# Two graph layers on one core: the additions X + H move from between the layers into layer two, and the offsets come first

## The chip, the cores and the metric

One core of a Trainium2 chip runs the whole program. The metric is the device time of one execution in microseconds (us); the kernel before takes 1938.24 us as the median of 3 runs (1938.19 to 1938.62).

## What is computed

3125 nodes with 160 features each (64 scalars, 32 vectors of three), 103125 edges sorted by target. Each of two layers does

```
h = relu(layernorm(x))
x = x + layer(h, edges)
```

Layer one makes a message per edge from the row h[src], the edge's four values and weights from a small network over 64 edge features, sums the messages by target, and applies node matrices and gates. Layer two is

```
out0 = C0 * (ss * e0 @ W1 + dot * INV3 @ W2)      # ss, vv: the rows h[src]
out1 = C1 * (p3 + p4 + p5)
m_agg = segment_sum(concat(out0, out1), dst)
x = x + relu([m_agg_s @ Ws, m_agg_v @ Wv])
```

What matters here is the residual of layer two: the result is X + H + relu(...) in the kernel's terms, where X is the sum after layer one without h, and H is relu(layernorm(X)), because layer two's own input h is added to its output.

## The kernel before, in words

All arithmetic is in float32. Nodes lie in 25 tiles of 128; `X` and `H` are 128 x 25 x 160 in SBUF. Edges are cut into 116 turns (the code's groups) of seven tiles of 128 edges, the last turn holding one. Four turns make an iteration; layer two runs two leading iterations (turns 0 to 7), written out, and then nine periods of three iterations.

For every edge tile the rows of the source nodes have to be brought into `g`. There are three ways. Most tiles are fetched from a table in HBM by an indirect DMA whose descriptors GpSimd (POOL) writes, from indices in SBUF (line 704, one per tile). Some seventh tiles are made by TensorE: VectorE compares node numbers with the wanted ones (lines 819 and 824, `compare`), TensorE multiplies the resulting 0/1 tiles with `H` (line 1003, `find`, 25 matmuls), ScalarE copies the result (line 745). A few are fetched row by row by SyncE and ScalarE (line 612).

In layer two a turn is then: VectorE builds the selection (lines 802 and 806, `select`), TensorE sums seven tiles (line 992, `aggregate`), VectorE turns the result (line 877, `turn`), and once in four turns TensorE applies the layer's matrix (line 1013, `lin2`) and VectorE adds to `acc` at an offset read from `place_i` (line 891, `accumulate`). The gather of turn s waits for the aggregation of turn s-4, the aggregation waits for its gathers in two parts (four tiles, then the rest), and `sel` has two buffers. VectorE's order in a stage is select, compare for two turns ahead, turn of the turn before, accumulate. If the targets of a turn span more than a window of 32 nodes, the layer is passed over again.

Between the layers (`vector_mid`, line 1097) VectorE, ScalarE, TensorE and POOL work tile by tile on layer one's node results (lines 1063, 1082, 1106, 1109, 1152, 1117), then statistics, roots and the normalised `H` (lines 1122, 286, 288, 1132, 1136 on VectorE; line 293 on ScalarE for tiles 0 to 11). SyncE writes `H` to the table in eight pieces as they come (line 1161), and POOL's first gather of layer two waits for all eight. VectorE goes on, after its last piece of `H`, with X = X + H in two parts (lines 1139 and 1141), the offsets of the windows (`windows`, lines 429, 432 and 433: `rel`, `place`, `place_i`), and the products of the weight tables (lines 1146 and 1147), for which TensorE waits before it composes layer two's matrix (line 1072). Then layer two begins on VectorE.

The tail (`vector_tail`, line 1174) adds relu of the aggregated result to `X` and stores it.

Of the kernel before, what the change touches and what calls it, by code (L numbers as in the profile page):

```python
# [28 lines left out]
ALU = mybir.AluOpType  # L29
# [4 lines left out]
P = 128  # L34
N = 3125
E = 103125
NT = -(-N // P)
# [40 lines left out]
ROOT_AT = (4, 10, 14)  # L78
ROOTS = (0, 18, NT)
BY_ACT = 12  # L80
PIECES = ((0, 2), (BY_ACT, 15), (2, 5), (15, 18), (5, 8), (18, 22), (8, BY_ACT), (22, NT))
THIRD = 3

# [18 lines left out]
def build(nc, x, node_vec, src_idx, src_rows0, src_rows1, src_by_row, node_id, dst_idx, edge_sh, edge_feat, ident, iota, lin_sc, lin_sc_scale,  # L102
# [7 lines left out]
    with ctx:  # L110
        def sb(name, shape, dt=F32):
            return ctx.enter_context(nc.sbuf_tensor(name, shape, dt))
# [4 lines left out]
        def sem(name):  # L117
            return ctx.enter_context(nc.semaphore(name))
# [6 lines left out]
        X = sb("X", [P, NT, D])  # L125
        H = sb("H", [P, NT, D])
# [15 lines left out]
        pool_sb = sb("pool_sb", [P, 2])  # L142
        eps_col = sb("eps_col", [P, 1])
        warm = sb("warm", [P, 1])
        ident_sb = sb("ident_sb", [P, P])
        iota_sb = sb("iota_sb", [P, WIN])
        node_id_sb = sb("node_id_sb", [P, NT])
# [79 lines left out]
        edge_set = sem("edge_set")  # L227
# [13 lines left out]
        h1_ready = sem("h1_ready")  # L241
        h1_by_dve = sem("h1_by_dve")
        scaled = sem("scaled")
        rows1_out = sem("rows1_out")
        added = sem("added")
        weights_ready = sem("weights_ready")
        comp_done = sem("comp_done")
        comp_copied = sem("comp_copied")
# [6 lines left out]
        by_dve = [tiles for tiles in pieces if tiles[0] >= BY_ACT]  # L255
# [170 lines left out]
        def windows(then):  # L426

            wide = [P, GROUPS, TILES]
            then(nc.vector.tensor_tensor(rel[:].rearrange("p (g t) -> p g t", t=TILES),
                                         dst[:].rearrange("p (g t) -> p g t", t=TILES),  # L430
                                         first[:].unsqueeze(2).to_broadcast(wide), ALU.subtract))
            then(nc.vector.tensor_copy(place[:], first[0:1, :]))
            then(nc.vector.tensor_copy(place_i[:], place[:]))
# [58 lines left out]
        def edge_layer(layer):  # L492
            L = f"l{layer}_"
            own_weights = layer == 0
# [298 lines left out]
            def vector(dve):  # L793
# [78 lines left out]
                def turn(f, o, s):  # L872
                    dve.wait_ge(agg_done, UNROLL * f + (o + 1))
                    if o % UNROLL == 0 and s != 0:

                        dve.wait_ge(lin2_done, f)
                    nc.vector.transpose(turned_all[:, o % UNROLL, 0:planes, :].rearrange("p c n -> p (c n)"),  # L877
                                        sums[:, o % 2, 0:width]).then_inc(turn_done, 1)
# [14 lines left out]
                def stage(f, it, o, s, p, e, k):  # L893
                    if s == 0:
                        dve.wait_ge(node_id_in, 16)
                        compare(f, p, e, PICKED[layer][0], 0, 0, True)
                    if s is None or s < GROUPS:
                        select(f, it, o, s)
                        if pick_after(o, s, p, 2):
                            compare(f, p, e, (o + 2) % UNROLL, *pick_after(o, s, p, 2), s is not None and s + 2 < UNROLL)  # L900
                        if s == GROUPS - 2:
                            accumulate(f, it, range(UNROLL), 0)
                        if own_weights:
                            products(f, it, o, 0, s, p, e)
                            if tiles_of(s) == TILES:
                                products(f, it, o, 1, s, p, e)
                            if o == UNROLL - 1 and s != GROUPS - 1:
                                if s == GROUPS - 1 - UNROLL:
                                    dve.wait_ge(named_in[layer], 16 * f + 32)
                                    dve.sem_inc(named_read, 1)  # L910
                                    dve.sem_inc(match_done, 1)
                                else:
                                    compare(f, p, e, 2, 0, 1, False)
                    if s is None or 1 <= s <= GROUPS:
                        turn(f, o - 1, None if s is None else s - 1)
                    if s == GROUPS:
                        nc.vector.tensor_scalar(rel[:], rel[:], float(WIN), None, ALU.subtract)
                        nc.vector.tensor_scalar(place[:], place[:], float(WIN), float(NPAD), ALU.add, ALU.min)
                    if o >= UNROLL:
                        if o == UNROLL + 1:  # L920
                            accumulate(f, it, range(UNROLL), 1)
                    elif o >= 2 and (s is None or UNROLL <= s < GROUPS - 2):
                        accumulate(f, it, range(2 * (o - 2), 2 * (o - 2) + 2), 0)

                with passes(dve) as r:
                    stages(dve, r, stage, GROUPS + 2)
                    pass_over(dve, r)

                    dve.drain()
                    nc.vector.tensor_copy(place_i[:], place[:])  # L930
                    dve.drain()

# [162 lines left out]
                nc.scalar.activation(big1_sb[:, m, :], banks[:, m % BANKS, 0:D], ACT.Copy).then_inc(comp_copied, 1)  # L1095

        def vector_mid(dve):
            n = 0
            for t in range(NT + 2):
                if t < NT:  # L1100
                    pre = banks[:, t % BANKS, :]
                    dve.wait_ge(node0_done, t + 1)
                    dve.wait_ge(sig_ready, t + 1)
                    if t >= BANKS:
                        dve.wait_ge(x_ready, t - BANKS + 1)
                    nc.vector.scalar_tensor_tensor(out=val[:, t % BANKS, 0:S_CH], in0=pre[:, 0:S_CH],
                                                   scalar=a_col[:, t:t + 1], in1=sig[:, t % BANKS, 0:S_CH],
                                                   op0=ALU.mult, op1=ALU.mult)
                    nc.vector.scalar_tensor_tensor(
                        out=val[:, t % BANKS, S_CH:D].rearrange("p (c i) -> p c i", i=3),  # L1110
                        in0=pre[:, S_OUT:PRE].rearrange("p (c i) -> p c i", i=3), scalar=a_col[:, t:t + 1],
                        in1=sig[:, t % BANKS, S_CH:S_OUT].unsqueeze(2).to_broadcast([P, V_CH, 3]),
                        op0=ALU.mult, op1=ALU.mult).then_inc(val_ready, 1)
                u = t - 2
                if u >= 0:
                    dve.wait_ge(x_ready, u + 1)
                    last = nc.vector.bn_stats(stats[:, u, :], X[:, u, :])
                    if u == parts[n][-1]:
                        last.then_inc(stats1_step, 1)
                        dve.wait_ge(stats1_step, n + 1)  # L1120
                        for v in parts[n]:
                            last = nc.vector.bn_aggr(mean_var[:, v, :], stats[:, v, :])
                        last.then_inc(var1_step, 1)
                        n += 1
            n = 0
            for i, own in enumerate(by_dve):
                if n < len(parts) and own[-1] >= parts[n][0]:
                    invert(dve, parts[n], n, root1_done, norm1_step, norm1_ready)
                    n += 1
                    dve.wait_ge(norm1_ready, n)  # L1130
                for u in own:
                    last = nc.vector.tensor_scalar(H[:, u, :], X[:, u, :], rstd[:, u:u + 1], shift[:, u:u + 1], ALU.mult, ALU.add)
                last.then_inc(scaled, 1)
                dve.wait_ge(scaled, i + 1)
                at = slice(own[0], own[-1] + 1)
                nc.vector.tensor_scalar(H[:, at, :], H[:, at, :], 0.0, None, ALU.max).then_inc(h1_by_dve, 1)
            assert n == len(parts)
            dve.wait_ge(h1_by_dve, len(by_dve))
            nc.vector.tensor_tensor(X[:, BY_ACT:, :], X[:, BY_ACT:, :], H[:, BY_ACT:, :], ALU.add).then_inc(added, 1)
            dve.wait_ge(h1_ready, BY_ACT)  # L1140
            nc.vector.tensor_tensor(X[:, 0:BY_ACT, :], X[:, 0:BY_ACT, :], H[:, 0:BY_ACT, :], ALU.add).then_inc(added, 1)
            dve.wait_ge(acc1_clear, 2)
            then = Steps(dve, edge_set)
            windows(then)
            dve.wait_ge(pair_in, 64)
            nc.vector.tensor_tensor(pair[:], pair[:], pair_k[:], ALU.mult)
            nc.vector.tensor_tensor(wout[:], wout[:], wout_k[:], ALU.mult).then_inc(weights_ready, 1)
# [251 lines left out]
```

## Time and profile before

| | us |
|---|---|
| median of 3 runs | 1938.24 |
| lowest, highest | 1938.19, 1938.62 |
| the profiled execution's own time | 1939.32 |
| span of the trace | 1937.5 |
| TensorE busy (matmul) | 1791.9 |
| POOL busy | 1408.5 |
| VectorE busy | 1371.9 |

The trace's times count from the span's start. Layer one fills it up to about 1011 us, the part between the layers up to about 1045 us, layer two the rest. Busy time of POOL counts the writing of descriptors (0.95 us for a gather), not the 0.30 us that follows each.

### The profile page before, as it was taken

Reading aid. Unit: us, or ns where it says so; the run is one execution under the profiler, and the core shown is the slowest. Engines: PE = TensorE matmul, PEld = TensorE weight load, DVE = VectorE, ACT = ScalarE, POOL = GpSimd, SP = SyncE. Lnnn points to the kernel's source line nnn. Section 1 sums busy time; section 2 is a strip of 40 time slices with the busy share of each in tenths; the row PEclk is TensorE's granted clock in tenths of the full one; section 3 lists DMA queues with packets and bytes.
Section 4 is the critical chain, followed back from the end, with each engine's and each line's share of the span. In section 5 each row is a group of like instructions: output and inputs, shape, how many; then the busy total and the mean of one; then the engine's idle time right before and its main releaser. Section 6 shows DMA issues by size and latency. Waiting matters only on the chain.

```text
span 1937.5 us, 55467 instructions
## 1 busy us (share of the span) xinstructions
PE 1791.9 (92%) x16896; PEld 1559.4 (80%) x16896; DVE 1371.9 (71%) x2793; ACT 174.6 (9%) x402; POOL 1408.5 (73%) x1505
## 2 busy tenths in 40 slices
PE   6989889898989899898975999999999999999998
PEld 4767666676767676676654899999999999999998
DVE  5878787878787878787778556666565665656654
ACT  5100001010010001010122000000000000000000
POOL 1777777777777777777755777777777777777774
PEclk9999999999999989899986999999999999999999
DMA  6333333434334343434323333233333323333233
GB/s 239 103 101 104 103 104 103 104 93 109 98 103 105 103 104 103 105 92 114 102 70 82 77 73 77 72 77 73 77 75 73 76 72 76 73 76 76 73 77 91
DMA packets 110902, 179.67 MB, mean 93 GB/s; under 512 B 30046, under 2 KB 78460, under 8 KB 110460
## 3 DMA queue, kind: packets, MB, share of 16 engines
q0 software_dynamic: 70656, 120.68, 26.1%
q1 hardware_dynamic: 35288, 53.34, 8.7%
q10 hardware_dynamic: 4644, 2.19, 0.5%
q8 instruction: 108, 1.77, 0.4%
q14 instruction: 206, 1.69, 0.3%
HBM read 169.95 MB, written 6.14 MB: 91 GB/s over the span
## 4 chain that ended last, share of the span: by engine, by line
POOL 49%; PE 23%; issue 18%; DVE 4%; DMA 3%; ACTq 2%; DVEq 1%; POOLq 0%; ACT 0%
POOL g L704 49%; PE w_ps L1003 12%; PE sums L992 4%; PE sums L1013 2%; DMA g<-node_table,src 2%; ACTq L612 1%; DVE work L858 1%; PE sums L1003 1%; PE sums L988 1%; PE w_ps L956 1%; DVE work L852 1%; PE w_ps L481 1%; PE sums L460 1%; PE hid_ps L942 1%; ACTq L609 0%
## 5 line engine op out<-in xcount | busy, mean ns | idle before, releaser
L704 POOL DMA_INDIRECT g<-node_table,src x1472 | 1394.0, 947 | 479.7 <-issue 464.3
L1003 PE MATMUL w_ps<-H,work 128*128 128x160 f32 x2900 | 405.5, 300 | 1.5 <-issue 1.5
L1003 PEld LDWEIGHTS w_ps<-H,work 128*128 128x128 f32 x2900 | 399.2, 191 | 1.9 <-issue 1.9
L858 DVE TENSOR_TENSOR work<-w_ps,g 128x384 f32<-128x384 f32 (+3 forms) x693 | 297.8, 457 | 87.6 <-DMA g<-node_table,src 47.7
L956 PE MATMUL w_ps<-fc_sb,work 64*128 64x224 f32 x1612 | 238.0, 394 | 90.8 <-DVE work L852 78.4
L877 DVE STREAM_TRANSPOSE turned<-sums 128x160 f32<-128x160 f32 x232 | 79.3, 342 | 306.9 <-PE sums L1013 201.8
L988 PEld LDWEIGHTS sums<-work,sel 128*32 128x32 f32 x6448 | 203.6, 114 | 112.9 <-issue 70.1
L956 PEld LDWEIGHTS w_ps<-fc_sb,work 64*128 64x128 f32 x1612 | 172.7, 199 | 137.8 <-DVE work L852 104.8
L806 DVE TENSOR_TENSOR sel<-mixed,sh 128x896 f32<-128x896 f32 x232 | 251.4, 1084 | 26.6
L988 PE MATMUL sums<-work,sel 128*32 128x160 f32 x6448 | 255.5, 311 | 0.0
L992 PE MATMUL sums<-g,sel 128*128 128x160 f32 x1612 | 237.5, 301 | 6.6 <-DMA g<-node_table,src 4.9
L992 PEld LDWEIGHTS sums<-g,sel 128*128 128x128 f32 x1612 | 224.7, 190 | 10.0 <-DMA g<-node_table,src 3.8
L824 DVE TENSOR_TENSOR work<-mixed,node_id_sb 128x3200 f32<-128x3200 f32 x58 | 202.5, 3491 | 4.5
L824 DVE TENSOR_TENSOR acc<-mixed,node_id_sb 128x3200 f32<-128x3200 f32 x55 | 192.0, 3491 | 8.6 <-PE w_ps L1003 4.6
L1003 PE MATMUL sums<-H,acc 128*128 128x160 f32 x1400 | 198.1, 302 | 0.0
L1003 PEld LDWEIGHTS sums<-H,acc 128*128 128x128 f32 x1400 | 191.8, 191 | 7.9 <-issue 7.9
L1003 PE MATMUL w_ps<-H,acc 128*128 128x160 f32 x1350 | 187.8, 299 | 0.0
L1003 PEld LDWEIGHTS w_ps<-H,acc 128*128 128x128 f32 x1350 | 184.2, 190 | 0.0
L852 DVE TENSOR_TENSOR work<-w_ps,g 128x256 f32<-128x256 f32 x462 | 155.7, 377 | 0.0
L942 PE MATMUL hid_ps<-feat,fc_sb 128*128 128x512 f32 x232 | 145.5, 712 | 1.5 <-issue 1.5
L1013 PE MATMUL sums<-turned,big_sb 128*80 128x128 f32 (+1 forms) x1044 | 125.8, 275 | 0.9 <-DVE turned L877 0.9
L1013 PEld LDWEIGHTS sums<-turned,big_sb 128*80 128x80 f32 (+1 forms) x1044 | 116.6, 156 | 8.5 <-issue 7.0
(85 smaller groups left out, 650.1 us busy)
## 6 DMA issues: line engine op xcount, KB each, us to landing
g<-node_table SPq DMA_DIRECT2D x2304, 0.6 KB
feat<-edge_feat_dram SPq DMA_DIRECT2D x60, 512.0 KB
g<-node_table,src POOLq DMA_INDIRECT x1472
g<-node_table ACTq DMA_DIRECT2D x1152, 0.6 KB
named<-src_rows_dram SPq DMA_DIRECT2D x30, 192.0 KB
X<-x_dram SPq DMA_DIRECT2D x5, 400.0 KB, 7.1
node_table<-H SPq DMA_DIRECT2D x5, 400.0 KB, 2.7
named<-src_rows_dram SPq DMA_DIRECT2D x30, 64.0 KB
```

What stands on the lines that cost most here:

```text
L704: nc.gpsimd.indirect_dma_start(out=g[:, slot(p, u, j), :], out_offset=None, in_=table[layer], in_offset=bass.IndirectOffsetOnAxis(ap=src[: ...
L806: nc.vector.tensor_tensor(sel[:, o % 2, 0:n, :].rearrange("p t (k n) -> p t k n", k=4), hot[:, 0:n, :].unsqueeze(2).to_broadcast([P, n, 4, ...
L824: nc.vector.tensor_tensor(match[layer][i], wanted.unsqueeze(1).to_broadcast(wide), node_id_sb[:].unsqueeze(2).to_broadcast(wide), ALU.is_e ...
L852: return nc.vector.tensor_tensor(blocks(at), w[:, :, h * S_CH:(h + 1) * S_CH].rearrange("p t (m c) -> p t m c", m=2), rows[:, :, 0:S_CH].r ...
L858: nc.vector.tensor_tensor(blocks(at), w[:, :, 2 * S_CH + j * V_CH:2 * S_CH + (j + 1) * V_CH].unsqueeze(2).to_broadcast([P, n, m, V_CH]), r ...
L877: nc.vector.transpose(turned_all[:, o % UNROLL, 0:planes, :].rearrange("p c n -> p (c n)"), sums[:, o % 2, 0:width]).then_inc(turn_done, 1)
L942: nc.tensor.matmul(hid_ps[:], fc1_sb[:], feat[:, half, within * HID:(within + 1) * HID], start=True, stop=True).then_inc(hid_done, 1)
L956: last = nc.tensor.matmul(w_ps[:, h, part[2 * h + j] - a, 0:W_N], hid[at, o % 2, (2 * h + j) * P:(2 * h + j + 1) * P], fc2_sb[at, :], tile ...
L988: last = nc.tensor.matmul(sums[at, o % 2, 0:width].rearrange("p (m n) -> p m n", n=WIN), sel[:, o % 2, j, at], row, tile_position=(0, k * ...
L992: last = nc.tensor.matmul(sums[:, o % 2, 0:D], sel[:, o % 2, j, :], g[:, slot(p, o % UNROLL, j), :], **first_last)
L1003: last = nc.tensor.matmul(found_at[:, i, 0:D], match[layer][i][:, t, :], H[:, t, :], start=(t == 0), stop=(t == NT - 1))
L1013: last = nc.tensor.matmul(lin_ps[:, r, :].rearrange("p (u n) -> p u n", n=WIN), big[:, m, r * rows_of:(r + 1) * rows_of], turned_all[:, :, ...
```

## The change

`windows` is moved from the end of `vector_mid` to its start, followed by a memset of a new 128 x 1 tile `once` to 1. The two additions and their waits leave `vector_mid`. In layer two's stages 5 (tiles 12 to 24) and 6 (tiles 0 to 11), behind `turn`, VectorE does X = H * once + X with one scalar_tensor_tensor each. At the end of every pass over layer two `once` is set to 0, so that a second pass would add nothing.

```diff
+X_AND_H = {5: range(BY_ACT, NT), 6: range(BY_ACT)}
...
                     if s is None or 1 <= s <= GROUPS:
                         turn(f, o - 1, None if s is None else s - 1)
+                    if not own_weights and s in X_AND_H:
+                        tiles = X_AND_H[s]
+                        if tiles[0] == 0:
+                            dve.wait_ge(h1_ready, BY_ACT)
+                        else:
+                            dve.wait_ge(h1_by_dve, len(by_dve))
+                        dve.wait_ge(once_set, 1)
+                        nc.vector.scalar_tensor_tensor(out=X[:, tiles[0]:tiles[-1] + 1, :], in0=H[:, tiles[0]:tiles[-1] + 1, :],
+                                                       scalar=once[:, 0:1], in1=X[:, tiles[0]:tiles[-1] + 1, :],
+                                                       op0=ALU.mult, op1=ALU.add).then_inc(added, 1)
...
                     dve.drain()
+                    if not own_weights:
+                        nc.vector.memset(once[:], 0.0).then_inc(once_set, 1)
                     nc.vector.tensor_copy(place_i[:], place[:])
                     dve.drain()
...
         def vector_mid(dve):
+            windows(Steps(dve, edge_set))
+            nc.vector.memset(once[:], 1.0).then_inc(once_set, 1)
             n = 0
...
-            dve.wait_ge(h1_by_dve, len(by_dve))
-            nc.vector.tensor_tensor(X[:, BY_ACT:, :], X[:, BY_ACT:, :], H[:, BY_ACT:, :], ALU.add).then_inc(added, 1)
-            dve.wait_ge(h1_ready, BY_ACT)
-            nc.vector.tensor_tensor(X[:, 0:BY_ACT, :], X[:, 0:BY_ACT, :], H[:, 0:BY_ACT, :], ALU.add).then_inc(added, 1)
             dve.wait_ge(acc1_clear, 2)
-            then = Steps(dve, edge_set)
-            windows(then)
             dve.wait_ge(pair_in, 64)
```

## Rows read from the trace of the kernel before

**Rows 1.** Chain that ended last, 1036 to 1100: start us, us, what
```profile
1036.82 2.94 DMA node_table<-H
...
1040.60 1.68 POOL g L704
...
1096.56 2.53 DMA g<-node_table,src
1099.13 0.90 PE sums L992 x2
```

**Rows 2.** Line 704 from 1040 to the end: duration ns min/median/max, first and last start
```profile
L704 POOL DMA_INDIRECT g<-node_table,src x703: 942/946/1682, 1040.6 to 1919.3; - x176
  issue: 212.5, 697
```

**Rows 3.** PE timeline: start, us, engine, line, operation [idle before <- releaser]
```profile
1044.70 5.67 PE L1072 MATMUL w_ps<-wout,pair 128*128 128x160 f32 x20 [17.74 <-DVE wout L1147]
...
1081.82 2.17 PE L992 MATMUL sums<-g,sel 128*128 128x160 f32 x14 [1.74 <-DMA g<-node_table,src]
...
1096.80 1.32 PE L992 MATMUL sums<-g,sel 128*128 128x160 f32 x8 [1.93 <-DMA g<-node_table,src]
```

**Rows 4.** PE timeline, the end of layer two
```profile
1918.15 3.97 PE L992 MATMUL sums<-g,sel 128*128 128x160 f32 x28
1922.33 0.51 PE L992 MATMUL sums<-g,sel 128*128 128x160 f32 x2 [0.21 <-DMA g<-node_table,src]
```

**Rows 5.** Windows: us, PE, PEld, DVE, ACT, POOL busy, PE clock, DMA share, GB/s
```profile
1098.00:1105.00 7.00, 6.00 (x23) 5.87 (x23) 6.10 (x8) 0.00 (x0) 5.48 (x6) 0.51 0.31 74
```

**Rows 6.** Timeline, from layer one to the part between the layers
```profile
1011.00 0.21 DVE L930 CAST place_i<-place 1x116 int32<-1x116 f32 x1 [0.20 <-DVE acc L891]
1011.22 0.87 PE L1063 MATMUL w_ps<-ident_sb,acc 96*128 96x96 f32 x8 [2.25 <-DVE acc L891]
...
1012.09 0.28 DVE L1106 SCALAR_TENSOR_TENSOR val<-w_ps,a_col,sig 128x64 f32<-128x64 f32 x1 [0.88 <-PE w_ps L1063]
```

**Rows 7.** VectorE's timeline, the end of the part between the layers
```profile
1029.52 0.33 DVE L1117 BATCH_NORM_STATS2 stats<-X 128x6 f32<-128x160 f32 x1 [0.17 <-POOL X L1152]
...
1036.83 2.33 DVE L1139 TENSOR_TENSOR X<-X,H 128x2080 f32<-128x2080 f32 x1
1039.07 2.15 DVE L1141 TENSOR_TENSOR X<-X,H 128x1920 f32<-128x1920 f32 x1
1041.14 1.00 DVE L429 TENSOR_TENSOR rel<-dst,first 128x812 f32<-128x812 int32 x1
...
1042.66 1.49 DVE L1146 TENSOR_TENSOR pair<-pair,pair_k 128x1280 f32<-128x1280 f32 x1
1044.07 0.48 DVE L1147 TENSOR_TENSOR wout<-wout,wout_k 128x320 f32<-128x320 f32 x1
```

**Rows 8.** POOL's third gather of layer two
```profile
1043.83 1.13 POOL L704 DMA_INDIRECT g<-node_table,src  x1 [0.30 <-issue]
```

**Rows 9.** Timeline in layer one: POOL's first gather, and one beside a product in SBUF
```profile
38.66 1.30 POOL L704 DMA_INDIRECT g<-node_table,src  x1 [20.50 <-issue]
...
47.46 1.14 DVE L441 TENSOR_TENSOR big_sb<-big_sb,work 128x960 f32<-128x960 f32 x1
47.77 1.66 POOL L704 DMA_INDIRECT g<-node_table,src  x1 [0.30 <-issue]
```

**Rows 10.** VectorE's timeline where the additions are put (stages 5 and 6)
```profile
1086.28 0.35 DVE L877 STREAM_TRANSPOSE turned<-sums 128x160 f32<-128x160 f32 x1 [4.40 <-PE sums L1013]
...
1088.37 3.49 DVE L824 TENSOR_TENSOR work<-mixed,node_id_sb 128x3200 f32<-128x3200 f32 x1
1094.91 0.35 DVE L877 STREAM_TRANSPOSE turned<-sums 128x160 f32<-128x160 f32 x1 [3.04 <-PE sums L992]
```

**Rows 11.** Memset of a 128 x 1 tile on VectorE
```profile
0.81 0.06 DVE L386 MEMSET eps_col<- 128x1 f32 x1 [0.67 <-PEq L1392]
```

**Rows 12.** PE timeline behind the waits of turn 6
```profile
1109.71 2.06 PE L992 MATMUL sums<-g,sel 128*128 128x160 f32 x14
```

More of the change, by code:

```diff
@@ L144, in build @@
         warm = sb("warm", [P, 1])
+        once = sb("once", [P, 1])
         ident_sb = sb("ident_sb", [P, P])
@@ L245, in build @@
         added = sem("added")
+        once_set = sem("once_set")
         weights_ready = sem("weights_ready")
```

## The prediction

> **What bounds the kernel now.** I read the chain of waits first, in the stretch where the change is, then each engine's timeline on both sides of the seam, then the end. The chain runs from VectorE's last piece of H over its write to the table (2.94 us, landed at 1039.76) to POOL's first gather 0.84 us later at 1040.60, along POOL's gathers for 56 us, and over the landing of one of them at 1099.13 to TensorE [rows 1]. The additions, the offsets and the weight products of VectorE are not in it. The reader should then see that POOL never stops in layer two: 703 gathers start from 1040.60 to 1919.35, (1919.35 - 1040.60) / 702 = 1.25 us apart, each 0.95 us long with 0.30 us behind it, and the idle time before them is put down to issue 697 times [rows 2]. TensorE is nearly as full, but in the first turns it is the one that waits: it comes to the aggregation of turn 4 and finds the rows missing for 1.74 us, and again in turn 6, for 1.93 us and once more up to the landing at 1099.13 [rows 1, 3]. From there it has no idle time up to the end, where turn 114 is summed by 1918.15 + 3.97 = 1922.12 and the single tile of turn 115 waits 0.21 us for its landing [rows 4]. So the end is set by POOL: its start in layer two, plus 703 gathers, plus a tail. TensorE has about 0.2 us to spare there, and its own chain is tied to POOL's at turn 6 too.
>
> **The change, part by part.**
>
> 1. The additions and the offsets leave the place ahead of the weight products. The products start at 1042.66 and now could start at 1036.83, 5.83 us sooner but for the delay of part 2 [rows 7]. TensorE waits 17.74 us for them [rows 3], so its composing, its first find and its first aggregations come about 5 us sooner. This is worth nothing: at turn 4 TensorE waits already, the 5 us are added to that wait, and from turn 4 it goes at the time of POOL's landings as before. Cover: the missing rows. The next thing late is again a gather.
>
> 2. The offsets at the start of the part between the layers. VectorE ends the cast of line 930 at 1011.21 and starts line 1106 at 1012.09, 0.88 us later [rows 6]. The offsets take 1042.66 - 1041.14 = 1.52 us for the three operations with their waits [rows 7], and the memset 0.06 us [rows 11]: 1.58 us in a gap of 0.88 us, so at least 0.70 us is left over. VectorE also has to close its loop before them; what of the gap this takes isn't shown, and it lies between 0 and 0.88 us. TensorE's first transposes start 0.22 us after the cast begins, about 0.4 us after the last addition that they wait for [rows 6]; the nearest row is of that size, so I take 0.3 us. Sum: +1.0 us, ends 0.7 and 1.6. Nothing takes it back: from 1012.09 to the last of H at 1036.8 VectorE's only listed gap is 0.17 us [rows 7]. All of H, SyncE's eight writes and POOL's first gather move with it: 1040.60 to 1041.6. ScalarE and TensorE wait for VectorE tile by tile here and move too.
>
> 3. The first gathers lose two neighbours. The first of layer two took 1.68 us, beside line 1141 and line 429 [rows 1, 7], the first of layer one 1.30 us [rows 9]; the third of layer two took 1.13 us, begun under line 1146, against 0.95 us [rows 7, 8]. In the changed order VectorE is through with its products at about 1037.8 + 1.9 = 1039.7, before the first gather. Gain 0.38 + 0.18 = 0.56 us; 0.9 us if the first gather falls to 0.95 us, nothing if it was slow for another reason.
>
> 4. The additions in stages 5 and 6. On VectorE they cost 2.33 + 2.15 us (lines 1139 and 1141 have the same shapes and types [rows 7]). VectorE idles 4.40 us before the turn of stage 5 and 3.04 us before that of stage 6 [rows 10]. The first addition pushes select and the comparison back by 2.33 us into the 3.04 us gap, so the turn of stage 6 is on time. The second pushes accumulate, select and the comparison behind it by about 2.2 us; the selection of turn 7 would be done at about 1101 (1094.9, the turn's 0.35, 2.15, and some 3 us for the two steps behind), and TensorE wants it at 1109.7 [rows 12]. Queued behind on SyncE are the next row numbers and row fetches, some 2 us later with many turns to go. As VectorE time the price is nothing, covered by these gaps.
>
> The price is on POOL. Line 441, a product with both inputs in SBUF (by its tiles: big_sb and work), ends at 47.46 + 1.14 = 48.60. The gather begun at 47.77 takes 1.66 us in place of 0.95: 0.71 us longer, as if it had stood still from 47.89 to 48.60 [rows 9]. The third gather of layer two is 0.18 us longer, and line 1146, again two inputs in SBUF, ends at 1044.15: still from 1043.97 [rows 7, 8]. Both give one picture: 0.12 to 0.14 us after its start a gather needs something that such an operation holds to its end. The comparison of line 824, 3.49 us long with one input in PSUM, does not do it: the gathers under it keep 0.95 us, which is all but the whole of the median in rows 2. Both additions have their two large inputs in SBUF, and POOL is in the midst of its gathers. An addition of length T stops the first gather that comes to that point within it, for T less a part of the 1.25 us period: 1.08 to 2.33 us for the first, 0.90 to 2.15 us for the second. I take the middles, since where it falls is a matter of tenths: 1.7 + 1.5 = 3.2 us, ends 2.0 and 4.5. No stop at all is a rival below. TensorE is shifted alike, as both delayed gathers come before the landings of turn 6 that it waits for.
>
> The Trainium skill says of this, in "SBUF — State Buffer", section "Who interferes with whom", that a VectorE instruction with two SBUF inputs contends with a GpSimd instruction that reads SBUF; the rows of lines 441 and 1146 agree. The same section says that a tensor_tensor was not seen to stall a DMA, inferring that descriptors need only the write side; by that part 4 would be nothing and the sum would be +0.4 us.
>
> 5. At the end of the pass, a memset of 0.06 us ahead of the last cast, when VectorE has no work but waits for TensorE's transposes: nothing; at worst 0.06 us.
>
> Sum: +1.0 - 0.56 + 3.2 = +3.6 us. Ends: 0.7 - 0.9 + 2.0 = +1.8 and 1.6 - 0.56 + 4.5 = +5.5. Against the profiled execution: its span 1937.5 becomes 1941.1 and its own time 1939.32 becomes 1942.9. The median shown is 1.1 us under that time, so 1938.24 becomes 1941.8, between 1940.0 and 1943.7.
>
> **The rivals.**
>
> No stop. The scalar_tensor_tensor isn't a tensor_tensor and may not hold what the gathers need, or short stalls may be made up. For it: only a few rows show the stall at all, and none with this operation. Against: two stalls fit one picture to 0.02 us, and POOL has no pause in which to make anything up. Time: +1.0 - 0.56 = +0.4 us, 1938.7.
>
> Slower: a second slow stretch of TensorE. Its clock is at 0.51 (the lower level, 1.2 GHz) from 1098 to 1105, behind the waits of turn 6 [rows 5]; that costs it about 7.0 x 0.49 = 3.4 us. The change lengthens these waits, by 5 us before turn 4 and by 3 us in turn 6. A slow stretch before turn 6 is hidden, since rows are missing there anyway. Behind turn 6 TensorE has 0.2 us to spare: if the low clock lasts one stretch longer there, the end moves by nearly all of it: +3.6 + 3.4 = +7.0 us, 1945.2. Against: before, too, the clock fell once after such waits and then stayed up.
>
> Faster: the 5 us of part 1 reach the end, with the offsets' 1.0 us already in them: 5.8 - 1.0 = 4.8 us, 1933.4. This needs TensorE to be the bound from the start. Against: the waits in turns 4 and 6 and POOL's 703 gathers without a pause.
>
> **How the numbers follow.** A measurement of this kernel can tell about 0.2% (3.9 us) from no change. The forecast has 0.68, no stop 0.17, the slow stretch 0.11, the faster case 0.04. The forecast's own range, 1940.0 to 1943.7, straddles the bound at 1942.1: about 0.41 of it (0.28) lies above. So slower is 0.28 + 0.11 = 0.39, same 0.40 + 0.17 = 0.57, faster 0.04. The range takes in the forecast's and the case without a stop, 1938.2 to 1944.0; it leaves out the two others and a little more.
>
> **What would show it.** The first gather of layer two near 1041.6 and near 1.3 us long; line 1072 about 5 us sooner, the wait before turn 4's aggregation near 6 us; two gathers of 2 to 3.3 us near 1088 and 1096, each beside an addition, and no others; 1.25 us between all the rest; the last gather near 1923. It is wrong if these two gathers keep 0.95 us (then +0.4 us), if POOL's first gather comes before 1041.0 or after 1042.4, or if TensorE is still summing well after the last landing.

## The result, and the profile after

| | before | after |
|---|---|---|
| median of 20 runs, us | 1938.22 | 1941.29 |
| lowest, highest | 1936.81, 1940.08 | 1939.92, 1943.26 |
| span of the trace | 1937.5 | 1938.6 |

The change makes the kernel 3.07 us slower: ratio 1.0016, 95% interval 1.0010 to 1.0022. That is clear of no change, though under the 3.9 us that the prediction set as its bound between slower and the same. Single executions differ by 3 us, so the spans of two traces can't be subtracted: in the trace after, layer one ended 1.72 us sooner (the cast of `place_i` at 1009.28, in [rows 6] at 1011.00). I compare from that cast.

The seam after, VectorE's timeline (start, us, engine, line, operation [idle before]); it answers to [rows 6]:

```profile
1009.28 0.21 DVE L945 CAST place_i<-place 1x116 int32<-1x116 f32 x1 [0.20 <-DVE acc L894]
1009.73 1.00 DVE L432 TENSOR_TENSOR rel<-dst,first 128x812 f32<-128x812 int32 x1 [0.24 <-issue]
...
1011.28 0.06 DVE L1114 MEMSET once<- 128x1 f32 x1
1011.35 0.28 DVE L1123 SCALAR_TENSOR_TENSOR val<-w_ps,a_col,sig 128x64 f32<-128x64 f32 x1
```

The first tile starts 2.07 us after the cast began, before 1.09: the offsets cost 0.98 us. The 0.24 us ahead of line 432 is the loop's end. Everything up to POOL's first gather keeps this distance: the gather comes 30.58 us after the cast, before 29.60.

The end of the part between the layers on VectorE, to [rows 7], and the first and third gather of POOL, to [rows 1, 8]:

```profile
1035.98 1.48 DVE L1157 TENSOR_TENSOR pair<-pair,pair_k 128x1280 f32<-128x1280 f32 x1
1037.38 0.48 DVE L1158 TENSOR_TENSOR wout<-wout,wout_k 128x320 f32<-128x320 f32 x1
1040.68 0.29 DVE L822 CAST mixed<-named 128x128 f32<-128x128 int32 x1 [2.82 <-DMA named<-src_rows_dram]
```

```profile
1039.86 1.19 POOL L707 DMA_INDIRECT g<-node_table,src  x1 [11.11 <-DMA node_table<-H]
...
1042.60 0.95 POOL L707 DMA_INDIRECT g<-node_table,src  x1 [0.30 <-issue]
```

The products end before the first gather starts; it takes 1.19 us (before 1.68) and the third 0.95 (before 1.13). VectorE now waits 2.82 us for row numbers.

Layer two where the additions stand, VectorE and POOL together, to [rows 10]:

```profile
1089.17 0.35 DVE L880 STREAM_TRANSPOSE turned<-sums 128x160 f32<-128x160 f32 x1 [12.28 <-PE sums L1028]
1089.44 2.35 DVE L926 SCALAR_TENSOR_TENSOR X<-H,once,X 128x2080 f32<-128x2080 f32 x1
...
1090.10 2.51 POOL L707 DMA_INDIRECT g<-node_table,src  x1 [0.30 <-issue]
...
1093.55 3.49 DVE L827 TENSOR_TENSOR work<-mixed,node_id_sb 128x3200 f32<-128x3200 f32 x1
...
1094.16 0.94 POOL L707 DMA_INDIRECT g<-node_table,src  x1 [0.30 <-issue]
...
1098.07 2.17 DVE L926 SCALAR_TENSOR_TENSOR X<-H,once,X 128x1920 f32<-128x1920 f32 x1
...
1099.16 1.90 POOL L707 DMA_INDIRECT g<-node_table,src  x1 [0.30 <-issue]
```

This is the answer. A gather begun inside each addition takes 2.51 and 1.90 us in place of 0.95, and ends 0.82 us after the addition does (1092.61 behind 1091.79, 1101.06 behind 1100.24; the ends are start plus duration), as the gather of [rows 9] ended 0.83 us behind line 441. The gathers under the comparison, one input in PSUM, keep 0.94 us. No other gather of the layer is over 1.19 us. Short operations hardly matter: in this trace some 40 gathers come to the same point, 0.12 us after their start, while VectorE is in line 894, `acc` and `lin_sb`, both inputs in SBUF but only 64 columns and about 0.2 us long, and they take 0.94 to 1.00 us.

Line 707 from 1030 to the end (duration min/median/max, first and last start), to [rows 2], and TensorE's timeline at the end, to [rows 4]:

```profile
L707 POOL DMA_INDIRECT g<-node_table,src x703: 942/946/2509, 1039.9 to 1920.5; - x176
```

```profile
1919.23 3.97 PE L1007 MATMUL sums<-g,sel 128*128 128x160 f32 x28
1923.43 0.51 PE L1007 MATMUL sums<-g,sel 128*128 128x160 f32 x2 [0.24 <-DMA g<-node_table,src]
```

POOL is still without a pause, and TensorE still waits 0.24 us for the last landing.

TensorE's early turns, to [rows 3], and the clock's windows, to [rows 5] (us, busy of PE, PEld, DVE, ACT, POOL, then the granted clock):

```profile
1038.01 4.49 PE L1087 MATMUL w_ps<-wout,pair 128*128 128x160 f32 x20 [11.79 <-DVE wout L1158]
1044.56 8.72 PE L1018 MATMUL w_ps<-H,work 128*128 128x160 f32 x50 [2.06 <-DVE work L827]
...
1078.96 2.50 PE L1007 MATMUL sums<-g,sel 128*128 128x160 f32 x8 [3.88 <-DMA g<-node_table,src]
1082.83 1.97 PE L1007 MATMUL sums<-g,sel 128*128 128x160 f32 x6 [1.36 <-DMA g<-node_table,src]
```

```profile
1044.00:1054.00 10.00, 9.44 (x57) 9.45 (x58) 6.99 (x7) 0.30 (x1) 7.56 (x9) 0.83 0.38 87
...
1078.00:1090.00 12.00, 9.67 (x43) 9.27 (x44) 0.83 (x2) 0.38 (x1) 9.05 (x10) 0.57 0.30 70
1090.00:1130.00 40.00, 38.46 (x284) 37.73 (x283) 27.72 (x28) 1.59 (x5) 30.88 (x30) 1.00 0.29 70
```

TensorE composes 28.73 us after the cast, before 33.70: 5 us sooner. It gives them back: its first find runs partly at the lower level (mean clock 0.83; 8.72 us in place of 7.05), and at turn 4 it waits 3.88 and 1.36 us for rows. The slow stretch has moved: it comes behind the wait of 3.88 us and lasts until about 1089 (0.57), and TensorE waits for rows again after it, so it is hidden; behind turn 6 there is none.

The sum from the two traces, cast to last gather, is 1920.54 - 1009.28 = 911.26 us after against 1919.35 - 1011.00 = 908.35 before: +2.91 us of the measured +3.07. It is made of +0.98 (offsets), -0.50 and -0.19 (distance from the first gather to the second 1.49 for 1.99, third to fourth 1.25 for 1.44), +1.56 and +0.96 (the two stops): +2.81. Of the other 0.10 us, 0.09 lies in the short pauses between the gathers (214.07 us in all for 213.98); why is not shown.

### The profile page after: what moved, and what is told of

Same layout as the page of the kernel before. It is cut to its first block, busy times and chain, and to the rows that moved or that the text cites. A ratio compares the mean times of both kernels' runs of the same rounds, so it can differ in the third digit from the quotient of the medians.

```text
span 1938.6 us, 55471 instructions
## 1 busy us (share of the span) xinstructions
PE 1793.8 (93%) x16896; PEld 1556.9 (80%) x16896; DVE 1373.1 (71%) x2795; ACT 174.7 (9%) x402; POOL 1410.5 (73%) x1505
## 3 DMA queue, kind: packets, MB, share of 16 engines
q8 instruction: 108, 1.77, 0.4%
## 4 chain that ended last, share of the span: by engine, by line
POOL 51%; PE 20%; issue 19%; DVE 4%; DMA 3%; ACTq 3%; POOLq 0%; DVEq 0%; ACT 0%
POOL g L707 51%; PE w_ps L1018 12%; PE sums L1007 4%; ACTq L615 2%; DMA g<-node_table,src 2%; PE sums L1028 2%; DVE work L861 1%; ACTq L612 1%; PE w_ps L484 1%; DVE work L855 1%; DMA g<-node_table 0%; PE sums L1018 0%; DMA node_table<-H 0%; DVE val L1123 0%; POOLq L698 0%
```

## The experiments

Theory: layer two ends when POOL ends, and the additions cost what they stop of its gathers; the offsets cost their part not hidden in VectorE's gap. Rivals: VectorE's own time is what costs; the offsets are hidden; TensorE's clock does it. No run is aimed at the clock; against it stand the mean granted clocks, 0.960 before and after, and 0.962 and 0.961 in the two traces of experiment B at this pace, whose times lie 40 us apart.

**A. Parts undone.** The first eight runs fell on two chips where the kernel before itself took 3065.51 and 3114.78 us: there TensorE stood idle for issue for over 700 us at a mean granted clock of 0.81 to 0.82, and POOL waited for it (402 us before 75 of the gathers in the first trace). POOL doesn't set the end there. Their times can't test this theory, but VectorE's and POOL's rows between the layers and beside single operations do.

Without the additions:

```diff
-                    if not own_weights and s in X_AND_H:
-                        ...
```

> The changed kernel without X + H (both additions are left out, so layer two's residual lacks H; everything else stands). Stall theory (the additions cost only what they stop POOL's gathers, 1.56 and 0.96 us in the profile of the changed kernel): no gather over 1.3 us in layer two but the first, POOL's first to last start 880.68 - 2.52 = 878.2 us apart, time 2.5 us under the changed kernel, about 1938.8. Rival (the cost is VectorE's time or TensorE's slow stretch, the longer gathers are a symptom): POOL's stretch shrinks but the time stays within 1 us of the changed kernel's.

3063.29 us against 3065.51, ratio 0.9986 (0.9971 to 1.0000); the expectation needs a chip on which POOL sets the end. In its trace, and in that of its repetition below, the two long gathers are gone; the only one over 1.02 us is the first, 1.19.

The offsets back behind H:

```diff
         def vector_mid(dve):
-            windows(Steps(dve, edge_set))
-            nc.vector.memset(once[:], 1.0).then_inc(once_set, 1)
...
             dve.wait_ge(acc1_clear, 2)
+            windows(Steps(dve, edge_set))
+            nc.vector.memset(once[:], 1.0).then_inc(once_set, 1)
             dve.wait_ge(pair_in, 64)
```

> The changed kernel with the offsets back behind H, ahead of the weight products; the additions stay in layer two. Theory: the 0.98 us between line 930's cast and the first of the tiles goes back to 0.88 us after it, POOL starts 1.0 us sooner relative to layer one's end, the products still end before POOL's first gather; two gathers are stopped as before by 1 to 2.3 and 0.9 to 2.2 us. Time about 1.0 us under the changed kernel, 1940.3. Rival (the offsets at the start are hidden in VectorE's gap and the whole 3 us are the additions'): no change against the changed kernel.

3061.65 us, ratio 0.9984 (0.9973 to 0.9995): no verdict on the time. The seam answered: the first tile 1.10 us and the first gather 29.65 us after the cast, within 0.05 us of before the change (1.09 and 29.60). The two gathers beside the additions took 2.95 and 2.49 us.

Both again:

> Again the changed kernel without X + H (both additions are left out), since on the chip of the first four runs every kernel was paced by TensorE's gaps and not by POOL. Theory: no gather over 1.3 us in layer two but the first, POOL's first to last start 878.2 us apart (880.68 with the additions), time 2.5 us under the changed kernel and +0.5 us against the kernel before: the offsets' 1.0 us less the 0.5 to 0.7 us that the first gathers no longer lose. Rival (the additions cost as VectorE time): POOL's stretch shrinks, the time stays at +3 us.

> Again the changed kernel with the offsets back behind H; the additions stay in layer two. Theory: line 1123's first start 0.88 us after the cast of place_i as before, two gathers stopped by 0.9 to 2.3 us each, time about +2.0 us against the kernel before (1.0 less than the changed kernel's +3.1). Rival (the offsets are hidden): +3.1.

The second chip was slower still: 3110.72 us (0.9992, 0.9983 to 1.0001) and 3107.90 us (0.9979, 0.9969 to 0.9989) against 3114.78. The seams repeat: 30.58 us from cast to gather with the offsets first, 29.60 with them back; the gathers beside the additions took 2.62 and 2.49 us.

The offsets alone, from the kernel before:

```diff
         def vector_mid(dve):
+            windows(Steps(dve, edge_set))
...
-            then = Steps(dve, edge_set)
-            windows(then)
```

> The kernel before with nothing but the offsets moved to the start of the part between the layers; X + H stays behind H. Theory: the first tile starts 1.8 us after the cast of place_i and not 0.88, POOL's first gather comes 1.0 us later, no gather inside layer two is stopped, time +1.0 us (+0.7 to +1.3) against the kernel before. Rival (hidden in VectorE's gap, or won back since TensorE's weight products come 1.5 us sooner): 0 or under.

3114.88 against 3114.78 us, ratio 1.0002 (0.9993 to 1.0011), which can't tell 1 us, the size of the forecast. Its timeline at the seam (VectorE) and at the first gathers:

```profile
1740.72 0.21 DVE L930 CAST place_i<-place 1x116 int32<-1x116 f32 x1 [0.20 <-DVE acc L891]
...
1742.69 0.28 DVE L1107 SCALAR_TENSOR_TENSOR val<-w_ps,a_col,sig 128x64 f32<-128x64 f32 x1
```

```profile
1769.67 2.15 DVE L1142 TENSOR_TENSOR X<-X,H 128x1920 f32<-128x1920 f32 x1
...
1771.20 1.68 POOL L704 DMA_INDIRECT g<-node_table,src  x1 [11.11 <-DMA node_table<-H]
```

1.97 us from cast to tile: the offsets alone cost 0.88 us, the memset with its signal the other 0.10. The first gather comes 30.48 us after the cast. With the additions back in front of it, it takes 1.68 us again; in every trace of the changed kernel and its variants, where they are not there, it takes 1.19. The addition beside it ends 0.62 us after the gather's start, here (1771.82) as before (1041.22); less the 0.13 us that a gather runs first, this makes the 0.49 us. The operation behind the addition is a different one in the two kernels. So those 0.49 us were the additions'. The weight products, again beside gathers here, lengthen the second to 1.26 us, as they did the third in [rows 8]. What the offsets alone cost in time is not shown by any run where POOL sets the end: their 0.98 us rest on the seams and on the sum of the two traces.

The additions left out, now on a chip where the kernel before takes 1940.11 us:

> Once more the changed kernel without X + H (both additions are left out), to time it where POOL sets the end. Theory, if the kernel before runs at about 1938 us here: +0.5 us against it, 2.5 us under the changed kernel. If all kernels run above 3000 us as on the two chips so far, TensorE's gaps set the end and the additions, 2.5 us of POOL's time, should not be seen: within 5 us of the kernel before.

1940.62 us, ratio 1.0005 (0.9995 to 1.0014): +0.51 us where +0.5 was expected. That is 2.6 us under the changed kernel's +3.07, near the stops' 2.52, but the two differences are from different chips and their intervals (1.0010 to 1.0022, here 0.9995 to 1.0014) overlap, so it fits the theory and doesn't prove it. Its trace missed one figure of the expectation: POOL's first to last start are 878.87 us apart, not 878.2. The ordinary gathers average 946.7 ns there for 945.7 in the changed kernel's trace; over 702 of them that is the 0.7 us. The rival that the lost time is VectorE's own is not excluded by this run, since it takes away both; the next runs separate them.

**B. The stop by itself, 24 times.** The same operation, with its output to a tile that layer two doesn't use, at the place of stage 5 in every iteration of the loop; and its twin, which reads one of the inputs from PSUM (`steps`, 32 columns of `mixed`, read over and over):

```diff
+                    if not own_weights and s is None and o == 1:
+                        nc.vector.scalar_tensor_tensor(out=spare, in0=H[:, 0:BY_ACT, :], scalar=zero[:, 0:1],
+                                                       in1=X[:, 0:BY_ACT, :], op0=ALU.mult, op1=ALU.add)
```

```diff
+                        wide = spare.rearrange("p t (k n) -> p (t k) n", n=WIN)
+                        nc.vector.scalar_tensor_tensor(out=wide, in0=steps.unsqueeze(1).to_broadcast([P, BY_ACT * D // WIN, WIN]),
+                                                       scalar=zero[:, 0:1], in1=X[:, 0:BY_ACT, :].rearrange(...),
+                                                       op0=ALU.mult, op1=ALU.add)
```

> The changed kernel plus 24 more of such operations in layer two's loop (128 x 1920, both inputs in SBUF, the output to a free tile), one every four turns at the place of stage 5. Theory: each stops one gather by 2.17 us less a part of 1.25 us: 0.9 to 2.2 us each, about 1.5, together 22 to 52 us, about 37; 24 gathers in the loop last 1.9 to 3.1 us. Rival (a gather is stopped only by accident of the start, or VectorE's idle time covers it all): within 3 us of the changed kernel. Second rival (VectorE's time is what costs): then the twin with one input in PSUM costs the same.

> The twin of the kernel with 24 more operations: the same place, number, size, type and output, but one of the two inputs is read from PSUM. Theory: no gather is stopped by them (all stay at 0.95 us), and the operations of about 2.2 us lie in VectorE's idle time: within 2 us of the changed kernel. Rival (VectorE's time or the writing of so much SBUF is what costs): as slow as the twin with both inputs in SBUF.

On the slow chip the first took 3035.23 us (0.9895, 0.9870 to 0.9919), the twin 3062.00 (0.9986, 0.9973 to 0.9999): the forecast of the time failed, with the wrong sign. The gathers did what was forecast: beside each of the 24 one of 1.87 to 2.93 us, beside the twin's 24 none.

> Again the changed kernel with 24 more operations of 128 x 1920 with both inputs in SBUF. On the first chip each of the 24 lay beside a gather of 1.9 to 2.9 us, and none of the 24 with one input in PSUM did, but POOL's time didn't set the end there. Theory: where POOL sets it, the 24 stops of about 1.3 us reach it: +22 to +45 us over the changed kernel, about +33, so 1963 to 1986. Rival (the end is not POOL's): under +10 us.

3074.46 us (0.9870, 0.9853 to 0.9887): the same again.

> Once more the changed kernel with 24 more operations of 128 x 1920 with both inputs in SBUF, now where the kernel before runs at about 1940 us and POOL sets the end. Theory: each stops one gather by 0.9 to 2.2 us, 1.3 us on average by the two slower chips: +32 us over the changed kernel, about 1975 (1965 to 1990). Rival (VectorE's idle time covers it): 1943 to 1950. On the slower chips the same kernel was 1.1 to 1.3% faster than the kernel before; if that is a matter of the 24 operations and not of those chips, it shows here too: about 1918.

> Once more the twin with one of the two inputs in PSUM. Theory: no gather stopped by them, the time of the changed kernel within 2 us, 1943 (1941 to 1945). Rival (VectorE's time or its writes cost): as slow as the twin with both inputs in SBUF.

Against 1938.72 us on one chip: 1981.94 us with both inputs in SBUF (3 executions), ratio 1.0223 (1.0203 to 1.0243); 1941.73 us for the twin, ratio 1.0016 (1.0005 to 1.0026), which is the changed kernel's own ratio. One of the 24 in each, VectorE and POOL, first both inputs in SBUF, then one in PSUM:

```profile
1154.70 2.18 DVE L932 SCALAR_TENSOR_TENSOR feat<-H,zero,X 128x1920 f32<-128x1920 f32 x1
...
1154.88 2.82 POOL L707 DMA_INDIRECT g<-node_table,src  x1 [0.30 <-issue]
```

```profile
1153.90 0.94 POOL L707 DMA_INDIRECT g<-node_table,src  x1 [0.30 <-issue]
...
1154.04 2.17 DVE L933 SCALAR_TENSOR_TENSOR feat<-mixed,zero,X 128x1920 f32<-128x1920 f32 x1
...
1155.15 0.95 POOL L707 DMA_INDIRECT g<-node_table,src  x1 [0.30 <-issue]
```

The mean durations of VectorE's 24 are the same to 0.01 us (2.18); what differs is the place of one input, and that the one in PSUM is a small tile read again and again. No run has such a small tile in SBUF; but in the traces before and after no gather beside an operation with one input in PSUM (lines 805, 809 and 827 after) is over 0.97 us, whatever its shape. So VectorE's time costs nothing here, and the stop costs its full length: the 24 long gathers hold 42.4 us more than 24 ordinary ones, POOL's first to last start lie 922.83 us apart in place of 880.68, 42.2 more, and the time rose by 43.2 us less the changed kernel's 3.1, 40.1 us, with some 4 us of uncertainty from three executions. Expected were 32: the average stop was 1.77 us and not 1.3. 21 of the 24 operations begin 0.09 to 0.23 us ahead of a gather, so that it loses nearly all their length. The other three begin 0.00 to 0.06 us ahead of one, which runs through in 0.94 to 0.95 us; the next is stopped by 0.81 to 0.85 us, and the operation itself takes 2.22 to 2.25 us for 2.18. The regular phase has a likely reason, which no run tests: TensorE now waits for landings (37.6 us from 1100 on), the turn behind which the operation stands follows the landing of a gather, and so the operation would keep its phase to POOL's beat. The twin's 24, where gathers aren't held back, begin from 0.29 us before a gather to 0.83 us after one.

**C. The same work in shorter pieces.**

```diff
+                        for t in range(0, BY_ACT, 3):
+                            nc.vector.scalar_tensor_tensor(out=spare[:, t:t + 3, :], in0=H[:, t:t + 3, :], scalar=zero[:, 0:1],
+                                                           in1=X[:, t:t + 3, :], op0=ALU.mult, op1=ALU.add)
```

> As the kernel with 24 more operations of 128 x 1920 with both inputs in SBUF, but each cut into four of 128 x 480 (0.6 us each, back to back, 2.4 to 2.6 us in all). Theory (a gather waits only for the end of the operation in progress and then goes ahead of the next, as the third gather of the kernel before did between lines 1146 and 1147): two gathers stopped for 0 to 0.6 us per set, about 0.3 each, so 24 x 0.6 = 14 us over the changed kernel, about 1957. Rival (the four hold as one): as slow as the uncut, about 1975 or more.

1946.62 us, ratio 1.0036 (1.0021 to 1.0051): +7.9 against the kernel before, about +4.8 over the changed one, where 14 was expected and 40 was the price uncut. Two of its sets:

```profile
1153.26 2.56 DVE L933 SCALAR_TENSOR_TENSOR feat<-H,zero,X 128x480 f32<-128x480 f32 x4
...
1153.41 1.34 POOL L707 DMA_INDIRECT g<-node_table,src  x1 [0.30 <-issue]
...
1155.05 0.96 POOL L707 DMA_INDIRECT g<-node_table,src  x1 [0.30 <-issue]
```

```profile
1184.33 2.56 DVE L933 SCALAR_TENSOR_TENSOR feat<-H,zero,X 128x480 f32<-128x480 f32 x4
...
1185.11 1.34 POOL L707 DMA_INDIRECT g<-node_table,src  x1 [0.30 <-issue]
...
1186.75 0.96 POOL L707 DMA_INDIRECT g<-node_table,src  x1 [0.31 <-issue]
```

The lengthened gather ends 0.82 us behind the end of the first piece (0.68 us into the set) or of the second (1.31 us): it waits for the end of one piece (at most 0.42 us here) and gets in before the next, although the set runs on for another 1.9 or 1.3 us. The gathers over 1.02 us beside the sets, 20 in all, hold 4.9 us, the time's 4.8 (with an interval of 3 us either way). The expectation counted two stopped gathers per set, and the second was never stopped. Part of that may be luck of the sizes: the pieces start 0.63 us apart, two of them 1.26 us, and POOL's beat is 1.25 us, so the gather behind a stopped one comes to its point just when another piece ends. Pieces of other lengths weren't tried.

## Why the prediction was right, step by step

Forecast 1941.8 us, measured 1941.29. The mechanism is the forecast's; that the figure is so close is in part luck, since the terms that were measured add up to 2.81 us and not to 3.6, and the two medians differ by 3.07.

- What bounds the kernel: shown. 24 stops of POOL came out in POOL's stretch one for one (42.2 us for 42.4) and in the time within its uncertainty, 24 stretches of VectorE did not come out at all.
- Part 1, TensorE's 5 us: they came (4.97 us from the cast) and were worth nothing. The wait at turn 4 was 3.88 + 1.36 us, not near 6, since the first find ran partly at the lower clock.
- Part 2, the offsets: 0.98 us for 1.0. The loop's end took 0.24 us (0.3 was assumed, by a row of another engine, which happened to be near).
- Part 3, the first gathers: -0.69 us for -0.56. The first one came down to 1.19 and not 1.30.
- Part 4, the stops: 2.52 us for 3.2. The mechanism and its size per operation were right, the phase was a guess at the middle: the gathers began 0.66 and 1.09 us after their addition, which makes 1.56 and 0.96 us. In the three other traces at this pace with the additions in place the pair is 1.38 and 0.95, 1.22 and 0.95, 1.05 and 0.94 us. So the term is 2.0 to 2.5 us, and the middle of a free phase was too high: the second stop is 0.94 to 0.96 in all four, near the prediction's lower end of 0.90. What sets the phase here is not shown. The places were missed too: counted from the cast, the gathers come at 80.8 and 89.9 us, 4 to 5 us later than "near 1088 and 1096", because the turn of stage 5 waits for line 1028, which TensorE ran at the lower level (granted clock 0.59 from 1084 to 1090; 4.48 us, before 2.35). POOL is in its gathers there as well, so the stops came all the same.
- Part 5: the memset stands at 1929.11, while VectorE waits for TensorE; nothing.
- No stop: refuted by both gathers and by 24 of 24.
- The slow stretch behind turn 6: did not come. The clock fell earlier, from about 1078, behind a wait of 3.88 us, and there it is hidden.
- The faster case: refuted; POOL's beat is unchanged.
- The chances: with the bound at 1942.1, 0.43 and not 0.41 of the forecast's range lies above it, which would shift 0.01 from same to slower.

The Trainium skill's two sentences, in "SBUF — State Buffer", section "Who interferes with whom": that a VectorE operation with two SBUF inputs contends with a GpSimd instruction that reads SBUF agrees with every trace here, and scalar_tensor_tensor does so too (2.51 us for 0.95). That a tensor_tensor was not seen to stall a DMA doesn't hold for these indirect gathers: line 441 added 0.71 us to one, and the additions of the kernel before 0.49 us to the first.

## What to carry to other kernels

Idle time of VectorE is not free while GpSimd is the engine that sets the end: before work is moved there, look at where its inputs lie and what POOL is doing at that moment. A long operation with both inputs in SBUF cost up to nine tenths of its length in POOL's time (1.96 of 2.18 us), the same with one input in PSUM nothing; where it can't be moved to a time without gathers, cutting it into pieces half as long as POOL's beat took most of the price off (4.8 us for 40). How much of that other lengths would save is open.

And a step put into "a gap" at a seam costs what sticks out of it, here 0.98 of 1.6 us, if the engine is on the chain right behind.

## What was not expected

- The steady phase of experiment B: the operation met the next gather at nearly the same point, here nearly the worst one (21 of 24). On the first slow chip it was steady too, at another point: 16 of 24 stopped gathers began 0.74 to 0.76 us after their operation.
- On the two slow chips the 24 operations with both inputs in SBUF made the kernel 1.1% and 1.3% faster (two executions each), while the twin, run on the first, changed it by 0.14%. TensorE's idle time for issue was 732 us with them on the first chip, 757 to 763 us without them or with the twin; on the second 758 against 789 to 792. That is 26 to 33 us less, and the time fell by 30 and 40 us. On the first chip, where the twin ran, it is gathers held back, not VectorE's work, that goes with fewer of TensorE's gaps; why, and what those gaps are, no run here shows.
